# Attention on one core: score products on two half arrays in pairs of heads, and the value products of a group in two bursts

## The chip, the cores and the metric

The kernel is one program on one core of a Trainium2 chip. The metric is the device time of one execution in microseconds (us), the median of several runs. A core has TensorE (matrix products into PSUM), VectorE (DVE), ScalarE (ACT), GpSimd (POOL) and SyncE (SP, which only issues transfers here). They run side by side and meet at semaphores.

## What is computed

Sixteen sequences of 512 tokens with 128 features pass through six residual layers: a small per-channel MLP, attention, the MLP again, routed experts, a gated scan, and the experts again. The change is in the attention layer (and in two details of how the MLP before it stores the keys). Cut to what matters, that layer is:

```python
q = (x @ Wq).reshape(B, S, 16, 8)      # 16 heads of 8 dimensions
k = (x @ Wk).reshape(B, S, 4, 8)       # 4 key heads, each shared by 4 query heads
v = (x @ Wv).reshape(B, S, 4, 8)
q, k = rope(q), rope(k)
att = softmax(causal(q @ k.T * 8 ** -0.5))
x = x + (att @ v) @ Wo
```

## The kernel before, in words

**Parts.** The MLP layer in front splits each fp32 q and k value into three bf16 parts (high, middle, low) and stores them in DRAM (`q_parts`, `k_parts`). A product of q and k is then the sum over all nine pairs of parts: `KQ` = 72 rows of contraction for a head of 8 dimensions. SP loads q three times below itself (line 770) and a copy of k whose rows pair with it (line 772).

**Steps.** `attention` runs over 16 sequences n and, in each, 4 groups g of 4 heads that share a key head. One (n, g) is a step of the loop `step`; there are 64. Every queue is written out by hand and is in order; what an engine has to wait for is a semaphore before the instruction. In a step TensorE works for three groups at once:

- **scores** (`scores`, lines 813 and 815) of the group three steps ahead. For each chunk c of 128 queries and each head: the product q·k over the (c+1)·128 keys that the chunk may see, then a product identity × mask that adds -1e38 to the part above the diagonal. These come in six tiles (`S_TILES`), over two PSUM tiles `at_s_ps` of two banks each. DVE reduces each tile to the negative row maximum (`maxima`, line 1024); tile k waits until tile k-2 is reduced.
- **less_max** (line 825), the group of this step: ten tiles (`X_TILES`) of k·q with keys on the partitions, 512 columns each, with two rows more in the contraction that subtract the maximum (74 rows). They alternate over two banks `at_x_ps`; ACT writes exp of a tile to `at_p` (line 936), and tile i waits until ACT has read tile i-2. POOL sets the entries above the diagonal to zero, every two tiles (line 991).
- **weigh** (line 840), the group one step back: values × probabilities, fp32, with 32 columns of the array for each of the four heads, 32 matrix instructions in one burst. It waits for POOL's last masking of that group.
- **max_rows** (line 848) transposes the maxima of the group two steps ahead; ACT copies, POOL splits them into two bf16 parts, and SP stores and loads them as the two extra rows (lines 777 and 779).
- one of `turn_output`, `turn_normal`, `project` (lines 279, 861, 868) for the output of two groups, over one bank `at_misc_ps`, whose reader is ACT or DVE. It has to be read before `max_rows` may write there again.

The places in the row of ten tiles are numbers: `S_BEFORE` says before which tile each score tile stands, `WEIGH_AT` = 2, `ROWS_AT` = 3, `MISC_AT` = 7 say behind which tile the other pieces stand. ACT and POOL have the same numbers in their loops.

## Time and profile before

| what | value |
|---|---|
| median of 3 runs | 1807.9 us (1804.65 to 1808.93) |
| the profiled execution | 1808.5 us, of which the span of the trace is 1806.8 us |
| mean granted TensorE clock | 0.923 |
| attention, in the trace | about 226 to 860 us |
| its steady part, 300 to 800 us | PE busy 483.3, DVE 357.7, ACT 322.8, POOL 199.1 us; clock 1.00 |

Times in rows are microseconds from the start of the span. PE rows are matrix products, PEld rows are loads of the stationary operand. A product's duration in the trace holds its way through the array as well, so that consecutive products overlap in the rows: what a product costs is the distance from its start to the start of the next one.

### The profile page before, as it was taken

The page shows a single profiled execution, that of the slowest core. Times are in us where ns is not written, and L with a number is a line of the kernel's source. Part 1 is how long each engine was busy: PE and PEld are TensorE (multiplying, and loading weights), DVE is VectorE, ACT ScalarE, POOL GpSimd, SP SyncE. Part 2 cuts the span into 40 slices and gives each one's busy share as a digit, 9 for nine tenths or more (in the row PEclk, how much of TensorE's full clock was granted, in tenths as well). Part 3 has the DMA queues.
Part 4 walks back from the last instruction along what each step waited for, and adds up shares of the span by engine and source line. Part 5 has one row for each costly group of instructions (what it writes and reads, how often), then busy time and mean ns, then how long its engine had stood idle before and what let it go on. Part 6 is the DMA issues. An engine that isn't in the chain of part 4 may idle for free. (4 is left out here: it accounts for less than half of the span.)

```text
span 1806.8 us, 38981 instructions
## 1 busy us (share of the span) xinstructions
PE 1556.2 (86%) x11698; PEld 1092.2 (60%) x11698; DVE 1269.5 (70%) x3160; ACT 1156.7 (64%) x2439; POOL 771.7 (43%) x1202
## 2 busy tenths in 40 slices
PE   3999589999999999997799269999977834999998
PEld 1445245555555555553355159999964524999997
DVE  3787367777777777772786657787768766777776
ACT  3788316666666666665587347877847623788775
POOL 2587614334333444333343456655302203665540
PEclk9999759999999999998899579999989856999999
DMA  5022331111111111100011311111001100111110
GB/s 140 23 70 62 92 75 41 39 43 42 43 43 43 43 42 40 38 19 2 12 36 35 105 28 39 39 32 29 21 1 32 40 24 21 51 49 46 46 44 23
DMA packets 72828, 76.49 MB, mean 42 GB/s; under 512 B 13040, under 2 KB 61488, under 8 KB 72752
## 3 DMA queue, kind: packets, MB, share of 16 engines
q1 hardware_dynamic: 64560, 58.77, 11.2%
q0 software_dynamic: 8192, 16.79, 3.5%
q8 instruction: 37, 0.61, 0.1%
q14 instruction: 39, 0.32, 0.1%
HBM read 51.40 MB, written 24.12 MB: 42 GB/s over the span
## 5 line engine op out<-in xcount | busy, mean ns | idle before, releaser
L1024 DVE TENSOR_REDUCE at_negmax<-at_s_ps 128x2 f32<-128x1024 f32 (+3 forms) x384 | 393.2, 1045 | 170.3 <-PE at_s_ps L815 167.4
L936 ACT ACTIVATE at_p<-at_x_ps 128x512 f32<-128x512 f32 x640 | 353.5, 591 | 158.0 <-PE at_x_ps L825 151.2
L991 POOL TENSOR_SCALAR_AFFINE_SELECT at_p<-at_p 128x256 f32<-128x256 f32 (+1 forms) x448 | 190.8, 438 | 347.5 <-ACT at_p L936 347.5
L1248 POOL DMA_INDIRECT e_x_in<-xn,e_row_c x256 | 259.6, 1014 | 146.0 <-issue 85.0
L813 PE MATMUL at_s_ps<-at_kr,at_qr 72*128 72x512 bf16 (+3 forms) x1024 | 252.9, 312 | 23.2 <-DMA at_kr<-k_parts 20.7
L825 PE MATMUL at_x_ps<-at_qr,at_kr 74*128 74x512 bf16 (+3 forms) x1024 | 235.7, 305 | 22.6 <-ACT at_p L936 12.9
L1369 DVE TENSOR_TENSOR e_hid_lo<-e_hid,e_hid_hi 128x512 fp32r<-128x512 f32 x256 | 177.4, 694 | 83.2 <-ACT e_hid_hi L1333 74.5
L815 PE MATMUL at_s_ps<-maskb,identb 128*128 128x128 bf16 x1024 | 202.1, 225 | 0.0
L1332 ACT ACTIVATE e_hid<-e_h_ps 128x512 f32<-128x512 f32 x256 | 154.7, 604 | 42.1 <-PE e_h_ps L1274 37.4
L840 PE MATMUL at_o_ps<-at_p,at_va 128*32 128x512 f32 (+3 forms) x2048 | 155.5, 445 | 1.6 <-POOL at_p L991 1.6
L1274 PE MATMUL e_h_ps<-e_x_hi,w_hi 128*128 128x256 f32 x512 | 156.6, 306 | 0.0
L1333 ACT ACTIVATE e_hid_hi<-e_h_ps 128x512 fp32r<-128x512 f32 x256 | 155.3, 607 | 0.0
L825 PEld LDWEIGHTS at_x_ps<-at_qr,at_kr 74*128 74x128 bf16 x1024 | 84.6, 98 | 114.7 <-ACT at_p L936 84.2
L813 PEld LDWEIGHTS at_s_ps<-at_kr,at_qr 72*128 72x128 bf16 x1024 | 102.8, 100 | 83.8 <-issue 20.9
L1274 PE MATMUL e_h_ps<-e_x_hi,w_lo 128*128 128x256 f32 x512 | 145.9, 285 | 0.0
L1274 PE MATMUL e_h_ps<-e_x_lo,w_hi 128*128 128x256 f32 x512 | 145.5, 284 | 0.0
L1284 PE MATMUL e_yt_ps<-e_hid_hi,w_lo 128*128 128x256 f32 x512 | 144.3, 282 | 0.0
L1284 PE MATMUL e_yt_ps<-e_hid_hi,w_hi 128*128 128x256 f32 x512 | 144.1, 282 | 0.0
L1284 PE MATMUL e_yt_ps<-e_hid_lo,w_hi 128*128 128x256 f32 x512 | 144.0, 281 | 0.0
L1325 ACT ACTIVATE e_x_hi<-e_t_ps 128x256 fp32r<-128x256 f32 x128 | 49.5, 386 | 135.2 <-PE e_t_ps L1263 124.3
L840 PEld LDWEIGHTS at_o_ps<-at_p,at_va 128*32 128x32 f32 x2048 | 60.8, 111 | 96.2 <-issue 83.1
L1302 PE MATMUL e_acc_ps<-e_hot,e_y_hi 128*128 128x512 f32 x256 | 111.7, 436 | 3.0 <-DVE e_hot L1388 3.0
(196 smaller groups left out, 3495.6 us busy)
## 6 DMA issues: line engine op xcount, KB each, us to landing
at_qr<-q_parts SPq DMA_DIRECT2D x192, 96.0 KB
k_parts<-m_kparts SPq DMA_DIRECT2D x48, 96.0 KB, 1.8
at_kr<-k_parts SPq DMA_DIRECT2D x64, 72.0 KB
xres<-in_x_dram SPq DMA_DIRECT2D x8, 512.0 KB, 7.6
xn<-m_n_xhat SPq DMA_DIRECT2D x16, 256.0 KB
e_x_in<-xn,e_row_c POOLq DMA_INDIRECT x256
xn<-sc_n_xhat SPq DMA_DIRECT2D x16, 256.0 KB
out_dram<-xres SPq DMA_DIRECT2D x16, 256.0 KB
```

Of the source, the lines that this page charges most:

```text
L813: pe.matmul(s_ps[k % 2][:, at:at + w], qr[u][0:KQ, q0:q0 + P], kr[u][0:KQ, g * T:g * T + w], start=True, stop=False)
L815: mm = pe.matmul(s_ps[k % 2][:, at + w - P:at + w], h["identb"][:], h["maskb"][:], start=False, stop=True)
L825: mm = pe.matmul(x_ps[i % 2][:, at:at + T - c * P], kr[u][0:KM, g * T + c * P:g * T + (c + 1) * P], qr[u][0:KM, q0 + c * P:q0 + T], start= ...
L840: mm = pe.matmul(o_ps[32 * j:32 * j + 32, c * P:T], va[u][:, c, g, :], p_sb[g % 2][:, i, at:at + T - c * P], start=(c == 0 and g % 2 == 0) ...
L936: a.activation(p_sb[g % 2][:, i, :], x_ps[i % 2][:], ACT.Exp, scale=SCALE).then_inc(x_read, 1)
L991: sel = gp.affine_select(out=part, in_=part, compare_op=ALU.is_ge, fill=0.0, base=0, pattern=[[0, n] for n in part.shape[1:-1]] + [[1, P]] ...
L1024: v.tensor_reduce(negmax[u][:, h0:h0 + len(heads), c], s_ps[k % 2][:, 0:len(heads) * pitch].rearrange("p (j w) -> p j w", w=pitch)[:, :, 0:w],
L1248: nc.gpsimd.indirect_dma_start(out=x_in[k][u][:], out_offset=None, in_=xn_dram, in_offset=bass.IndirectOffsetOnAxis(ap=row_c[k][:, u:u + 1 ...
L1274: mm = pe.matmul(h_ps[half][:, f, :], w1[:, k, at:at + P], x[k % 2][:], start=(j == 0), stop=(j == len(pairs) - 1))
L1284: mm = pe.matmul(yt_ps[:], w2[:, k, f * D:(f + 1) * D], x[k % 2][:, f, :], start=(f == 0 and j == 0), stop=(f == FC - 1 and j == len(pairs ...
L1333: a.activation(hid_hi[k % 2][:, half * HC:(half + 1) * HC, :], h_ps[half][:], ACT.Gelu).then_inc(gelu_done, 1)
L1369: v.tensor_tensor(hid_lo[k % 2][:, chunks, :], hid[half][:], whole(hid_hi[k % 2][:, chunks, :]), ALU.subtract).then_inc(hl_done, 1)
```

## The change

**Contraction of 48 rows, twice.** Of the nine pairs of parts it keeps six (high with all three, middle with two, low with one), so `KQ` is 48 and `KM` is 50. q is laid out so that the even heads of a group stand at partitions 0 to 49 and the odd ones at 64 to 113, and k stands in both places. A score product now names 48 rows of one half of the array (`HALF` = 64 rows), and products are issued in pairs, one head on each half, which write to two different banks.

**Masks.** The mask product of 128 rows and 128 columns of a head is replaced by two products of 64 rows and 64 columns (`selb` × `maskb`), issued in turn for the two heads of a pair.

**less_max** takes the half by the parity of the tile: even tiles on rows 0 to 49, odd ones on rows 64 to 113. The last two tiles hold heads (0, 2) and (1, 3) instead of (0, 1) and (2, 3).

**weigh** is split in two bursts of 16 instructions: chunks 0 and 3 (512 and 128 columns) behind tile 1, chunks 1 and 2 (384 and 256 columns) behind tile 4. The wait for POOL's masking stands ahead of the first. Before, all 32 stood behind tile 2.

**Other pieces.** `max_rows` moves from behind tile 3 to behind tile 1, ahead of the first burst; the `misc` piece from behind tile 7 to behind tile 8. ACT copies the output of the value products behind tile 4 instead of tile 2.

**Transfers.** SP issues eight loads for a group instead of four (24, 16 and 8 rows of q and 48 of k for each half), and two loads of the maxima instead of one. The bytes of a group go from 360 to 288 KB. The stored copies of k are three of the high part, two of the middle and one of the low.

```diff
-KQ = PARTS * PARTS * HD
+KEPT = [PARTS - j for j in range(PARTS)]
+KFIRST = [sum(KEPT[:j]) for j in range(PARTS)]
+KQ = sum(KEPT) * HD
 KM = KQ + 2
+HALF = P // 2
...
-for copy in range(PARTS):
-    sp.dma_start(k_dram[i * W + b].rearrange("(j c p) t -> c p j t", c=PARTS, p=KR)[copy],
-                 rot["k"]["parts"][b * KR:(b + 1) * KR]).then_inc(parts_out[W], 16)
+rows = k_dram[i * W + b].rearrange("(x p) t -> p x t", p=KR)
+for j, copies in enumerate(KEPT):
+    part = rot["k"]["parts"][b * KR:(b + 1) * KR, j, :]
+    sp.dma_start(rows[:, KFIRST[j]:KFIRST[j] + copies, :],
+                 part.unsqueeze(1).to_broadcast([KR, copies, T])).then_inc(parts_out[W], 16)
...
-          [[(2, 2 * i, 0), (2, 2 * i + 1, 256)] for i in range(GH // 2)]
+          [[(2, i, 0), (2, i + 2, 256)] for i in range(GH // 2)]
 NX = len(X_TILES)
-S_TILES = [(3, (0, 1), 512), (3, (2, 3), 512), (2, (0, 1), 512), (2, (2, 3), 512), (1, (0, 1, 2, 3), 256), (0, (0, 1, 2, 3), 128)]
+S_TILES = [(3, (0, 1)), (3, (2, 3)), (2, (0, 1)), (2, (2, 3)), (1, (0, 1, 2, 3)), (0, (0, 1, 2, 3))]
 NS = len(S_TILES)
 S_BEFORE = {0: 0, 2: 1, 3: 2, 5: 3, 7: 4, 8: 5}
 NG = NKV // 2
 DEN = 2 * HD
-WEIGH_AT, ROWS_AT, MISC_AT = 2, 3, 7
+WEIGH_AT, MISC_AT = (1, 4), 8
+WEIGH_CHUNKS = ((0, 3), (1, 2))
...
-    q = q_dram[n].rearrange("(r h) t -> r h t", h=NH)
+    q = q_dram[n].rearrange("(r g a s) t -> s g r a t", g=NKV, a=2, s=2)
     k = k_dram[n].rearrange("(r h) t -> r h t", h=NKV)
-    rows = PARTS * HD
-    for j in range(PARTS):
-        sp.dma_start(qr[u][j * rows:(j + 1) * rows, g * GH * T:(g + 1) * GH * T].rearrange("r (h t) -> r h t", h=GH),
-                     q[:, g * GH:(g + 1) * GH, :]).then_inc(qk_in[u][g], 16)
-    sp.dma_start(kr[u][0:KQ, g * T:(g + 1) * T], k[:, g, :]).then_inc(qk_in[u][g], 16)
+    for half in range(2):
+        for j, kept in enumerate(KEPT):
+            at = half * HALF + KFIRST[j] * HD
+            sp.dma_start(qr[u][at:at + kept * HD, g * 2 * T:(g + 1) * 2 * T].rearrange("r (a t) -> r a t", a=2),
+                         q[half, g, 0:kept * HD]).then_inc(qk_in[u][g], 16)
+        sp.dma_start(kr[u][half * HALF:half * HALF + KQ, g * T:(g + 1) * T], k[:, g, :]).then_inc(qk_in[u][g], 16)
 def maxima(n, u, r, g):
     sp.wait_ge(m2_done, n * NKV + g + 1)
     sp.dma_start(m_dram[u].rearrange("a r q -> r a q")[g * GH * C:(g + 1) * GH * C], m_parts[g % 2][:]).then_inc(m_stored, 16)
     sp.wait_ge(m_stored, (n * NKV + g + 1) * 16)
-    sp.dma_start(qr[u][KQ:KM, g * GH * T:(g + 1) * GH * T],
-                 m_dram[u].rearrange("a r q -> a (r q)")[:, g * GH * T:(g + 1) * GH * T]).then_inc(m_in[u][g], 16)
+    for half in range(2):
+        sp.dma_start(qr[u][half * HALF + KQ:half * HALF + KM, g * 2 * T:(g + 1) * 2 * T].rearrange("a (x t) -> a x t", x=2),
+                     m_dram[u].rearrange("a (g x s c) q -> s g a x (c q)", g=NKV, x=2, s=2)[half, g]).then_inc(m_in[u][g], 16)
...
-    c, heads, pitch = S_TILES[k]
+        pe.wait_ge(qk_in[u][g], (r + 1) * 2 * (PARTS + 1) * 16)
+    c, heads = S_TILES[k]
     w = (c + 1) * P
     after(pe, s_read, (n * NKV + g) * NS + k - 1)
-    for x, j in enumerate(heads):
-        q0, at = (g * GH + j) * T + c * P, x * pitch
-        pe.matmul(s_ps[k % 2][:, at:at + w], qr[u][0:KQ, q0:q0 + P], kr[u][0:KQ, g * T:g * T + w],
-                  start=True, stop=False)
-        mm = pe.matmul(s_ps[k % 2][:, at + w - P:at + w], h["identb"][:], h["maskb"][:], start=False, stop=True)
+    for a in range(len(heads) // 2):
+        pair = []
+        for half in (first, 1 - first):
+            rows = slice(half * HALF, half * HALF + KQ)
+            q0 = (g * 2 + (heads[0] + 2 * a) // 2) * T + c * P
+            pair.append((slice(half * HALF, (half + 1) * HALF), half * T + a * w))
+            pe.matmul(s_ps[k % 2][:, half * T + a * w:half * T + (a + 1) * w], qr[u][rows, q0:q0 + P],
+                      kr[u][rows, g * T:g * T + w], start=True, stop=False)
+        for x in range(2):
+            for rows, at in pair:
+                at += w - P + x * HALF
+                mm = pe.matmul(s_ps[k % 2][:, at:at + HALF], h["selb"][rows, x * P:(x + 1) * P],
+                               h["maskb"][rows, x * HALF:(x + 1) * HALF], start=False, stop=x == 1)
     mm.then_inc(s_full, 1)
 def less_max(n, u, r, g, i):
     if i == 0:
-        pe.wait_ge(m_in[u][g], r * 16 + 16)
+        pe.wait_ge(m_in[u][g], (r + 1) * 2 * 16)
     after(pe, x_read, (n * NKV + g) * NX + i - 1)
+    rows = slice(i % 2 * HALF, i % 2 * HALF + KM)
     for c, j, at in X_TILES[i]:
-        q0 = (g * GH + j) * T
-        mm = pe.matmul(x_ps[i % 2][:, at:at + T - c * P], kr[u][0:KM, g * T + c * P:g * T + (c + 1) * P],
-                       qr[u][0:KM, q0 + c * P:q0 + T], start=True, stop=True)
+        q0 = (g * 2 + j // 2) * T
+        mm = pe.matmul(x_ps[i % 2][:, at:at + T - c * P], kr[u][rows, g * T + c * P:g * T + (c + 1) * P],
+                       qr[u][rows, q0 + c * P:q0 + T], start=True, stop=True)
     mm.then_inc(x_full, 1)
-def weigh(n, u, g):
-    if g == 0:
-        pe.wait_ge(va_done, n + 1)
-    if g % 2 == 0:
-        after(pe, o_copied, n * NG + g // 2)
-    pe.wait_ge(p_masked, (n * NKV + g) * 5 + 5)
-    order = sorted((c, j, i, at) for i in range(NX) for c, j, at in X_TILES[i])
+def weigh(n, u, g, part):
+    if part == 0:
+        if g == 0:
+            pe.wait_ge(va_done, n + 1)
+        if g % 2 == 0:
+            after(pe, o_copied, n * NG + g // 2)
+        pe.wait_ge(p_masked, (n * NKV + g) * 5 + 5)
+    order = sorted((c, j, i, at) for i in range(NX) for c, j, at in X_TILES[i] if c in WEIGH_CHUNKS[part])
     for c, j, i, at in order:
         mm = pe.matmul(o_ps[32 * j:32 * j + 32, c * P:T], va[u][:, c, g, :], p_sb[g % 2][:, i, at:at + T - c * P],
-                       start=(c == 0 and g % 2 == 0), stop=(c == 3 and g % 2 == 1))
-    mm.then_inc(pv_done, 1)
+                       start=(c == 0 and g % 2 == 0), stop=(c == WEIGH_CHUNKS[1][1] and g % 2 == 1))
+    if part == 1:
+        mm.then_inc(pv_done, 1)
...
-if i == WEIGH_AT and g:
-    weigh(n, u, g - 1)
-elif i == WEIGH_AT and not is_first(n):
-    weigh(n - 1, 1 - u, NKV - 1)
-if i == ROWS_AT and ahead_rows is not None:
+if i == WEIGH_AT[0] and ahead_rows is not None:
     max_rows(*ahead_rows, use(n, g, True))
+if i in WEIGH_AT and g:
+    weigh(n, u, g - 1, WEIGH_AT.index(i))
+elif i in WEIGH_AT and not is_first(n):
+    weigh(n - 1, 1 - u, NKV - 1, WEIGH_AT.index(i))
...
-if i == WEIGH_AT and g == 0 and not is_first(n):
+if i == WEIGH_AT[0] and ahead_rows is not None:
+    copy_rows(ahead_rows[0], ahead_rows[3], use(n, g, True))
+if i == WEIGH_AT[1] and g == 0 and not is_first(n):
     copy_output(n - 1, 1)
-elif i == WEIGH_AT and g == 2:
+elif i == WEIGH_AT[1] and g == 2:
     copy_output(n, 0)
-if i == ROWS_AT + 1 and ahead_rows is not None:
-    copy_rows(ahead_rows[0], ahead_rows[3], use(n, g, True))
...
+scored = s_ps[k % 2][:].rearrange("p (s x) -> p s x", s=2)[:, :, 0:len(heads) // 2 * w]
+if len(heads) == 2:
+    out = negmax[u][:, h0:h0 + 2, c]
+else:
+    scored = scored.rearrange("p s (a w) -> p a s w", w=w)
+    out = negmax[u][:, h0:h0 + GH, c].rearrange("p (a s) -> p a s", s=2)
+v.tensor_reduce(out, scored, AX.X, ALU.max, negate=True).then_inc(s_read, 1)
...
+row, last = at % HALF, at % HALF == HALF - 1
+later = np.where(row[:, None] < np.arange(HALF)[None, :], f32(MASKED), f32(0))
+w["mask"] = np.concatenate([later, np.where(last[:, None], f32(MASKED), later)], 1)
+same = (row[:, None] == np.arange(HALF)[None, :]).astype(f32)
+none = np.zeros((P, HALF), f32)
+w["self"] = np.concatenate([same, none, np.where(last[:, None], f32(1), none), np.where(last[:, None], f32(0), same)], 1)
```

TensorE's queue, behind the first exp tiles of a step (rows ISA and REGISTER_ALU are waits). Before: the third tile (L825), the burst of value products (L840), the next score tile.

```order
L825 MATMUL at_x_ps<-at_qr,at_kr 128x512
L837 ISA
L840 MATMUL at_o_ps<-at_p,at_va 32x512 x4
L840 MATMUL at_o_ps<-at_p,at_va 32x384 x4
L840 MATMUL at_o_ps<-at_p,at_va 32x256 x4
L840 MATMUL at_o_ps<-at_p,at_va 32x128 x4
L286 REGISTER_ALU
L813 MATMUL at_s_ps<-at_kr,at_qr 128x384
```

Now: the first two tiles (L843), the transposed maxima (L868), half of the value products (L859), a score tile as one pair of products (L826) with its four mask products (L831).

```order
L843 MATMUL at_x_ps<-at_qr,at_kr 128x512 x2
L289 ISA
L868 MATMUL at_misc_ps<-pack,at_negmax 16x128
L856 ISA
L859 MATMUL at_o_ps<-at_p,at_va 32x512 x4
L859 MATMUL at_o_ps<-at_p,at_va 32x128 x4
L826 MATMUL at_s_ps<-at_kr,at_qr 128x512 x2
L831 MATMUL at_s_ps<-maskb,selb 128x64 x4
L289 REGISTER_ALU
L843 MATMUL at_x_ps<-at_qr,at_kr 128x512
```

The burst moved ahead by one tile and one score tile, is half as long, and has the transposed maxima in front of it.

TensorE's queue, end of a step. Before: tile 7 (L825), a `misc` piece (L279), and the first head of the last score tile, which three more such pairs of L813 and L815 and tiles 8 and 9 follow.

```order
L825 MATMUL at_x_ps<-at_qr,at_kr 128x384
L825 MATMUL at_x_ps<-at_qr,at_kr 128x128
L853 ISA
L279 MATMUL at_misc_ps<-pack,at_o_t 128x128 x4
L286 REGISTER_ALU
L813 MATMUL at_s_ps<-at_kr,at_qr 128x128
L815 MATMUL at_s_ps<-maskb,identb 128x128
```

Now: the second pair of heads of the last score tile, tile 8, the `misc` piece, tile 9.

```order
L826 MATMUL at_s_ps<-at_kr,at_qr 128x128 x2
L831 MATMUL at_s_ps<-maskb,selb 128x64 x4
L289 REGISTER_ALU
L843 MATMUL at_x_ps<-at_qr,at_kr 128x256 x2
L873 ISA
L282 MATMUL at_misc_ps<-pack,at_o_t 128x128 x4
L289 REGISTER_ALU
L843 MATMUL at_x_ps<-at_qr,at_kr 128x256 x2
```

Eight products of 128 columns became four of 128 columns and eight of 64, and the `misc` piece now stands between the last two exp tiles.

## Rows read from the trace of the kernel before

**Rows 1.** The page: busy time, and granted clock in 40 slices.

```profile
PE 1556.2 (86%) x11698; PEld 1092.2 (60%) x11698; DVE 1269.5 (70%) x3160; ACT 1156.7 (64%) x2439; POOL 771.7 (43%) x1202
...
PEclk9999759999999999998899579999989856999999
```

**Rows 2.** Stretches: length, busy PE, PEld, DVE, ACT, POOL (instructions), clock, DMA share, GB/s.

```profile
300.00:800.00 500.00, 483.34 (x4648) 277.37 (x4646) 357.69 (x420) 322.79 (x638) 199.14 (x515) 1.00 0.14 41
```

**Rows 3.** Waits from 305 to 705 us: in total, times, longest.

```profile
ACT at_p L936 <- PE at_x_ps L825: 101.9, 147, 2.5
PEld at_x_ps L825 <- ACT at_p L936: 56.1, 167, 0.9
```

**Rows 4.** Timeline of PE, one step of 405 to 414 us: start, length, line.

```profile
405.26 0.38 PE L813 MATMUL at_s_ps<-at_kr,at_qr 72*128 72x512 bf16 x1
405.48 0.22 PE L815 MATMUL at_s_ps<-maskb,identb 128*128 128x128 bf16 x1
...
407.16 0.38 PE L825 MATMUL at_x_ps<-at_qr,at_kr 74*128 74x512 bf16 x1
407.47 2.36 PE L840 MATMUL at_o_ps<-at_p,at_va 128*32 128x512 f32 x32
409.77 0.34 PE L813 MATMUL at_s_ps<-at_kr,at_qr 72*128 72x384 bf16 x1
...
412.91 0.60 PE L279 MATMUL at_misc_ps<-pack,at_o_t 128*128 128x128 f32 x4
413.35 0.22 PE L813 MATMUL at_s_ps<-at_kr,at_qr 72*128 72x128 bf16 x1
413.41 0.22 PE L815 MATMUL at_s_ps<-maskb,identb 128*128 128x128 bf16 x1
```

**Rows 5.** The same view: `project`, and the burst four steps later.

```profile
431.39 1.11 PE L868 MATMUL at_misc_ps<-pack,at_o_nt 128*128 128x128 f32 x8
...
444.45 2.36 PE L840 MATMUL at_o_ps<-at_p,at_va 128*32 128x512 f32 x32
```

**Rows 6.** The same view in the scan layer: products on 64 rows and 64 columns.

```profile
1358.76 0.59 PE L1456 MATMUL sc_y_ps<-sc_ts,bmat 64*64 64x512 f32 x1
1359.28 1.09 PE L279 MATMUL sc_xt_ps<-pack,sc_n_xhat 128*128 128x128 f32 x8
...
1389.50 0.59 PE L1455 MATMUL sc_tf_ps<-sc_fg,wlam 64*64 64x512 f32 x1
1389.50 0.59 PE L1456 MATMUL sc_y_ps<-sc_ts,bmat 64*64 64x512 f32 x1
1389.92 0.59 PE L1455 MATMUL sc_tf_ps<-sc_fg,wlam 64*64 64x512 f32 x1
```

**Rows 7.** Timelines of ACT and POOL, start of the same step as Rows 4.

```profile
405.24 2.17 ACT L936 ACTIVATE at_p<-at_x_ps 128x512 f32<-128x512 f32 x4 [0.53 <-PE at_x_ps L825]
...
406.49 0.64 POOL L991 TENSOR_SCALAR_AFFINE_SELECT at_p<-at_p 128x512 f32<-128x512 f32 x1 [0.67 <-ACT at_p L936]
```

**Rows 8.** Timeline, scan layer: eleven products of 8 columns, each with a load.

```profile
1384.48 1.29 PE L249 MATMUL sc_gate_ps<-pack,sc_xhat_t 128*128 128x8 f32 x11
```

**Rows 9.** Stretches, columns as in Rows 2: start of attention, and steps without scores.

```profile
256.00:268.00 12.00, 12.00 (x56) 6.93 (x55) 7.51 (x7) 6.66 (x13) 3.64 (x9) 0.50 0.08 25
268.00:272.00 4.00, 4.00 (x32) 1.17 (x33) 1.23 (x1) 0.81 (x2) 0.41 (x1) 0.62 0.08 27
...
826.80:830.20 3.40, 2.61 (x15) 1.14 (x15) 0.00 (x0) 3.33 (x8) 2.38 (x7) 1.00 0.00 0
830.20:833.60 3.40, 2.91 (x14) 0.80 (x18) 0.00 (x0) 2.08 (x4) 1.20 (x3) 0.59 0.02 5
```

**Rows 10.** Timeline of PE in those steps: two bursts of value products, with idle between.

```profile
823.46 2.36 PE L840 MATMUL at_o_ps<-at_p,at_va 128*32 128x512 f32 x32
...
828.60 0.80 PE L825 MATMUL at_x_ps<-at_qr,at_kr 74*128 74x256 bf16 x4
...
830.65 1.10 PE L825 MATMUL at_x_ps<-at_qr,at_kr 74*128 74x512 bf16 x2 [0.51 <-ACT at_p L936]
831.68 1.94 PE L840 MATMUL at_o_ps<-at_p,at_va 128*32 128x512 f32 x8
```

**Rows 11.** Timelines at the start of attention: SP's first and last loads, the maxima; PE.

```profile
228.14 1.16 SPq L770 DMA_DIRECT2D at_qr<-q_parts  x3
...
241.88 0.36 SPq L772 DMA_DIRECT2D at_kr<-k_parts  x1
248.53 0.33 SPq L777 DMA_DIRECT2D row_max<-at_m_parts  x1
251.03 0.23 SPq L779 DMA_DIRECT2D at_qr<-row_max  x1
...
256.01 1.06 PE L825 MATMUL at_x_ps<-at_qr,at_kr 74*128 74x512 bf16 x2
```

More of the change, by code:

```diff
@@ L707, in attention @@
         s = lambda n: sem(f"at_{n}")
-        qr = [t(f"qr{u}", [P, NH * T], BF16) for u in range(2)]
+        qr = [t(f"qr{u}", [P, NH // 2 * T], BF16) for u in range(2)]
         kr = [t(f"kr{u}", [P, NKV * T], BF16) for u in range(2)]
@@ L875, in step @@
                             if ahead is not None and i in S_BEFORE:
-                                scores(*ahead, S_BEFORE[i])
+                                scores(*ahead, S_BEFORE[i], i % 2)
                             less_max(n, u, r, g, i)
-                            if i == WEIGH_AT and g:
-                                weigh(n, u, g - 1)
-                            elif i == WEIGH_AT and not is_first(n):
-                                weigh(n - 1, 1 - u, NKV - 1)
-                            if i == ROWS_AT and ahead_rows is not None:
+                            if i == WEIGH_AT[0] and ahead_rows is not None:
                                 max_rows(*ahead_rows, use(n, g, True))
+                            if i in WEIGH_AT and g:
+                                weigh(n, u, g - 1, WEIGH_AT.index(i))
+                            elif i in WEIGH_AT and not is_first(n):
+                                weigh(n - 1, 1 - u, NKV - 1, WEIGH_AT.index(i))
                             if i == MISC_AT and g == 3:
@@ L896, in first @@
                         for k in range(NS):
-                            scores(*FIRST, g, k)
+                            scores(*FIRST, g, k, 0)
                         if g:
@@ L903, in flush @@
                     done = use(n, NKV - 1, False) + 1
-                    weigh(n, u, NKV - 1)
+                    for part in range(2):
+                        weigh(n, u, NKV - 1, part)
                     turn_output(n, 1, done)
@@ L1564, in program @@
         q_dram = dram("q_parts", [NB, PARTS * P, T], BF16)
-        k_dram = dram("k_parts", [NB, PARTS * 96, T], BF16)
+        k_dram = dram("k_parts", [NB, KQ * NKV, T], BF16)
         xn_dram = dram("xn", [NB * T, D], F32)
@@ L1633, in layouts @@
     w["pairsum"] = np.tile(np.eye(M, dtype=f32), (2, 2))
-    w["mask"] = np.where(at[None, :] > at[:, None], f32(MASKED), f32(0))
+    row, last = at % HALF, at % HALF == HALF - 1
[4 more added lines that the diff above has]
+    w["self"] = np.concatenate([same, none, np.where(last[:, None], f32(1), none), np.where(last[:, None], f32(0), same)], 1)
     w["iota"] = np.broadcast_to(np.arange(T, dtype=f32), (P, T))
```

14 lines of the change are left out of this document (5 added, 9 removed).

## Prediction, written before the changed kernel had run

> **What bounds it now.** I read the page first: TensorE (PE) has the largest busy share, and its clock is at full speed through the attention layer [rows 1]. In the steady part of that layer PE is busy 483 of 500 us, DVE 358, ACT 323 [rows 2], so PE's queue sets the pace. From one burst of value products to the same burst a sequence later it is 444.45 - 407.47 = 36.98 us, 9.25 us for each of four steps [rows 4, 5]. The table of waits says that it is not PE alone: PE waited for ACT to read a tile (56 us in 400), and ACT for PE (102 us) [rows 3]. They have two banks between them; while PE runs a burst of 2.30 us (407.47 to 409.77, [rows 4]), ACT has two tiles to read, 1.1 us.
>
> **PE's work in a step before.** Distances between starts [rows 4]: a score product costs 0.22 us for 512 columns (405.26 to 405.48) and 0.06 for 128 (413.35 to 413.41), and in proportion between. Four heads of 512, 384, 256 and 128 columns: 4 × 0.56 = 2.2. Sixteen masks of 128 columns: 0.93. Exp tiles, 5120 columns: 2.2. The burst: 2.30. The misc piece is 0.44 (412.91 to 413.35), in one of four steps eight products of 0.11 [rows 5], 0.55 on average; max_rows another 0.11. Sum 8.3, so 0.95 of 9.25 us is waiting.
>
> **What the pairs take away.** Two products on two halves cost as much as one if they run at once. The trace has this in the scan layer: products on the two row halves start in the same hundredth of a microsecond, and the next pair 0.43 us later, the time of one such product alone [rows 6]. They also used different columns; pairs that share all 128 columns are in no row. I take them as parallel: 2.2 becomes 1.1. Exp tiles keep their 2.2, since one tile has one half; about 0.1 of it lies beside products of the other half.
>
> **The masks.** Sixteen products of 128 columns become 32 of 64, in 16 rounds of two. Half of 0.058 is 0.027 a round if columns alone decide; 0.058 if a round cannot be shorter than today's 128-column product; at worst 0.11, the distance at which products of 8 columns follow each other when each has a fp32 load of 128 columns [rows 8]. The masks' bf16 loads kept up with 0.058 before, so the last is far. I take 0.04: 0.64 us a step (0.43 to 0.93; 1.8 at the far end).
>
> The Trainium skill (TensorEngine Tiling (Array Packing), Instruction Overhead) warns against this edit: a product has about 60 cycles of overhead, and a factor should not be taken from a dimension that is already small. By it 64 columns cost what one column does, 32 products one behind the other about 0.8 us, and in rounds of two 0.4; the sum would be 1778 or 1772 by the one or the other. No row here has a 64-column product.
>
> **Changes of mode.** Going from one division of the array to another costs a gap. From the last exp tile (407.16, 0.22 of columns) to the burst (407.47) there are 0.09 us [rows 4], and from 64-row products (1358.76, 0.43 of columns) to a full one (1359.28) also 0.09 [rows 6]. Before, a step had two (into and out of the burst). Now it has seven: halves to full for max_rows, full to burst, burst to halves, halves to burst, burst to halves, halves to full for misc, and back. 7 × 0.095 = 0.67 us against 0.19.
>
> PE's work after: 1.1 + 0.64 + 2.1 + 2.11 (the burst without its gaps) + 0.55 + 0.11 = 6.6, with the gaps 7.3 us.
>
> **What waits remain.** I laid the new order beside the durations, from the first score tile of a step. (a) Tile 1 waits until ACT has read tile 9 of the step before: ACT needs 0.54 us a tile (2.17 for four, [rows 7]) and PE now arrives 0.3 us sooner: 0.34. (b) max_rows stood three tiles in, now one; the bank's last reader (DVE's normalise behind the last reduction, or ACT's copy) and the reduction are only just done: 0.28. (c) The first burst waits for POOL's mask of tiles 8 and 9: POOL started about 0.15 us after ACT's second tile ended and took 0.64 [rows 7]. Before, that was over at 407.13, 0.3 us ahead of the burst. One tile and one score tile earlier it comes last, about 1.4 us into the step: 0.23. (d) Tile 4 waits for ACT, which got tiles 2 and 3 together behind the burst: 0.39. (e) Tile 7 and the last tiles: 0.1 to 0.3. Sum 1.37. The step is 7.3 + 1.37 = 8.65 us. The same walk for the queue before gives 9.17 where the trace has 9.25, so I use the difference, 0.52 us a step, 2.1 a sequence.
>
> Of what the halving frees (1.1 + 0.3 on the masks), 0.5 goes to gaps and 0.4 to waits that move to POOL, DVE and ACT.
>
> **The sum.** The steady part has 15 sequences (280 to 820 us): -31 us. The last three steps have no scores and take 8.2 us from burst to burst (823.46 to 831.68, [rows 10]); with two short bursts ACT idles less: -2. Start: 32 loads took 13.7 us to issue (228.14 to 241.88), 64 take 27 and end near 255.5; the store and load of the first maxima behind them take 2.5 us plus landing [rows 11], so the first exp tile comes near 259 instead of 256.0: +3. The following steps run at half clock, where PE's halved products save about as much: -3. SP in the steady part has 11 issues of about 0.4 us in 8.7: hidden; the maxima have a whole step of slack, and bytes fall. DVE reduces the same elements. Sum -33 us: 1808.5 - 33 = 1775, and the median stands 0.6 us beside the profiled execution, so 1775 for both.
>
> **Rivals.**
>
> *The clock falls (slower).* The clock was at 1.2 GHz from the start of attention while PE was busy without a break with 72- and 74-row products, and rose only with the first burst of fp32 value products on 128 rows [rows 9]; in a step without scores it fell again [rows 9], where PE had idle gaps of 0.5 us and its columns were busy 60% of the step (4.9 of 8.2 us, [rows 10]). So being busy was not enough to raise it, and a looser step lost it. After the change PE's columns are busy 6.6 of 8.65 us, 76%, mostly on 48 or 50 rows: between the 60% that lost the clock and today's 88%. A step at half clock would take about 13.5 us, 4.8 more; one in each sequence costs 15 × 4.8 = 72 us and the time is 1848. It decides from one such step in 2.3 sequences on, where it eats the gain. The short bursts, two in a step, speak against it. The Trainium skill (TensorE: Matmul & The Clock Gate, HAM oscillation) names long idle gaps between bursts as the cause; by that rule the clock stays up and the time is 1775, but the fall in rows 9 had no gap over 0.6 us before it, so I keep this case.
>
> *The halves do not run together*, because they share columns: the products keep 2.2, the masks take 32 × 0.04 = 1.3, and the gaps stay: the walk gives 9.55 us a step against 9.17, 60 × 0.38 = 23 us: 1831.
>
> *Loads bound the masks* at 0.11 a round: 1.76 us a step instead of 0.64. Some of it falls into the waits; the walk then gives 9.08 a step against 9.17, 15 × 4 × 0.09 = 5 us: 1803, no change.
>
> *More than that*: gaps lie inside waits, masks cost 0.03, and (b) and (c) are half as long. Then a step is 8.2 us against 9.17 and the time 1748. DVE (358/500 of 9.25 = 6.6 us) and ACT (6.0) allow it.
>
> **Numbers.** Forecast 1775, with 1756 to 1795 its own range: 0.55. More: 0.13. Load-bound masks or other losses that end within 0.3% (about what a measurement of this kernel can tell from no change, 5.4 us): 0.10. Serial halves: 0.08. Clock: 0.14. Range 1742 to 1820: it takes in the fast rival and the cheap end of the clock's. Faster 0.68, same 0.11, slower 0.21.
>
> **What would show it.** Two L826 products in the same hundredth of a microsecond, the next pair 0.22 behind: pairs are right; at twice that they are serial. Mask rounds 0.03 to 0.06 apart. Gaps of 0.09 at seven places. A sequence of 34.9 us instead of 37.0. The first burst released by POOL L991 or its mask, max_rows by DVE. A clock of 1.00 from 280 to 820; anything less there and the forecast fails on the clock. It also fails if the waits grow where I have 1.37.

## The result, and the profile after

The changed kernel took 1812.1 us (median of 20 runs, 1808.1 to 1816.5), the one before 1808.1 beside it (20 runs, 1803.2 to 1811.7). The ratio is 1.0025, with a 95% interval of 1.0017 to 1.0034: nothing gained, where 33 us were forecast. The profiled execution took 1812.2 us (span 1810.5; before 1808.5 and 1806.8).

The page of the changed kernel: busy time, clock in 40 slices, and the queue q8, which moves code (experiments 1 to 4 show that it is PE's):

```profile
PE 1465.9 (81%) x12722; PEld 1011.2 (56%) x12722; DVE 1261.6 (70%) x3160; ACT 1159.9 (64%) x2439; POOL 767.4 (42%) x1202
...
PEclk9999758999999999997899579999988856999999
...
q8 instruction: 85, 1.39, 0.3%
```

PE is busy 90 us less than in [rows 1], and the end has not moved. Queue q8 carried 85 packets of 16 KB; before it was 37 (0.61 MB). That queue was on the page of the kernel before as well, and no step of the prediction had read it.

Stretches of the changed kernel (columns as in [rows 2]):

```profile
300.00:364.00 64.00, 53.60 (x757) 28.43 (x753) 46.70 (x55) 43.68 (x86) 25.96 (x68) 1.00 0.15 37
364.00:373.50 9.50, 6.15 (x48) 2.29 (x45) 3.74 (x7) 2.85 (x7) 2.91 (x8) 0.64 0.12 32
373.50:440.00 66.50, 55.67 (x777) 29.24 (x774) 48.69 (x57) 45.67 (x90) 27.02 (x71) 1.00 0.14 35
```

Most of the time the clock is 1.00 as forecast, and PE is filled less than before. In between lies a stretch of 9.5 us in which the clock is lower and all engines do little. Timeline of PE there:

```profile
363.87 0.39 PE L843 MATMUL at_x_ps<-at_qr,at_kr 50*128 50x256 bf16 x2
364.19 0.66 PE L282 MATMUL at_misc_ps<-pack,at_o_t 128*128 128x128 f32 x4
364.78 0.39 PE L843 MATMUL at_x_ps<-at_qr,at_kr 50*128 50x256 bf16 x2
368.51 0.61 PE L826 MATMUL at_s_ps<-at_kr,at_qr 48*128 48x512 bf16 x2 [3.35 <-issue]
```

PE stands still for 3.35 us and its releaser is "issue": it waited for nothing that the profile shows. The place is the end of the body of PE's loop over two images (the trace has a compare-and-branch at 364.5, then at 440.1, 515.3, 590.6, 665.4 and 740.7; behind the first five PE idles 3.0 to 3.4 us, behind the last, which leaves the loop, it does not). The same in the table of waits from 305 to 705 us (in total, times, longest), against [rows 3]:

```profile
ACT at_p L957 <- PE at_x_ps L843: 130.7, 112, 3.9
...
PEld at_x_ps L843 <- ACT at_p L957: 64.4, 123, 0.6
...
PEld at_s_ps L826 <- issue: 28.2, 51, 3.7
...
PE at_s_ps L826 <- issue: 16.1, 5, 3.4
```

Sixteen microseconds in five waits of PE; before, no such wait was there. From within or just behind each of the five the granted clock was half for 3.4 or 6.8 us (366.5 to 373.3, 441.5 to 448.4, 516.6 to 523.5, 595.1 to 598.6, 666.8 to 673.7).

What the two together cost is in the distances between the first bursts of successive steps. Timeline of PE, two first bursts, four steps (a sequence) apart:

```profile
388.96 1.28 PE L859 MATMUL at_o_ps<-at_p,at_va 128*32 128x512 f32 x16 [0.18 <-POOL at_p L1012]
...
424.34 0.64 PE L859 MATMUL at_o_ps<-at_p,at_va 128*32 128x512 f32 x4 [0.18 <-POOL at_p L1012]
```

An undisturbed sequence is 424.34 - 388.96 = 35.38 us, 1.6 less than the 36.98 of [rows 4, 5]: without the stalls the 58 steps from the third on that still have scores would have been 22.9 us shorter than before. Around the first stall the two distances are 357.97 to 369.90 and 369.90 to 380.13, 11.93 + 10.23 us, where the steps without a stall take 8.68 + 8.68: 4.8 us more. At the other four it is 4.4, 4.6, 4.0 and 4.5, in all 22.4. Nearly the whole gain went there.

At the end, the last three steps (without scores) took 30.3 us from burst to burst, 25.4 before, at a mean clock of 0.74 against 0.91. At the start the first burst came 3.4 us earlier (265.53), but the clock fell again from 274.3 to 284.5 and took 3.1 us back.

### The profile page after: what moved, and what is told of

Its sections match the earlier page's. It is cut to its first block and busy times, and to the rows that moved or that the text cites. A ratio compares the mean times of both kernels' runs of the same rounds, so it can differ in the third digit from the quotient of the medians.

```text
span 1810.5 us, 41589 instructions
## 1 busy us (share of the span) xinstructions
PE 1465.9 (81%) x12722; PEld 1011.2 (56%) x12722; DVE 1261.6 (70%) x3160; ACT 1159.9 (64%) x2439; POOL 767.4 (42%) x1202
## 5 line engine op out<-in xcount | busy, mean ns | idle before, releaser
L1051 DVE TENSOR_REDUCE at_negmax<-at_s_ps 128x2 f32<-128x1024 f32 (+3 forms) x384 | 383.9, 1042 | 174.6 <-PE at_s_ps L831 174.2
L843 PE MATMUL at_x_ps<-at_qr,at_kr 50*128 50x512 bf16 (+3 forms) x1024 | 209.6, 308 | 81.4 <-ACT at_p L957 75.4
L826 PE MATMUL at_s_ps<-at_kr,at_qr 48*128 48x512 bf16 (+3 forms) x1024 | 174.7, 316 | 43.6 <-DMA at_kr<-k_parts 20.9
L859 PE MATMUL at_o_ps<-at_p,at_va 128*32 128x512 f32 (+3 forms) x2048 | 178.0, 469 | 14.1 <-POOL at_p L1012 13.9
L831 PE MATMUL at_s_ps<-maskb,selb 64*128 64x64 bf16 x2048 | 138.3, 194 | 0.0
L831 PEld LDWEIGHTS at_s_ps<-maskb,selb 64*128 64x128 bf16 x2048 | 111.2, 99 | 34.0 <-issue 7.5
L843 PEld LDWEIGHTS at_x_ps<-at_qr,at_kr 50*128 50x128 bf16 x1024 | 60.3, 95 | 121.1 <-ACT at_p L957 103.3
L859 PEld LDWEIGHTS at_o_ps<-at_p,at_va 128*32 128x32 f32 x2048 | 56.6, 114 | 111.7 <-issue 89.5
```

Of the source, the lines that this page charges most:

```text
L826: pe.matmul(s_ps[k % 2][:, half * T + a * w:half * T + (a + 1) * w], qr[u][rows, q0:q0 + P], kr[u][rows, g * T:g * T + w], start=True, sto ...
L831: mm = pe.matmul(s_ps[k % 2][:, at:at + HALF], h["selb"][rows, x * P:(x + 1) * P], h["maskb"][rows, x * HALF:(x + 1) * HALF], start=False, ...
L843: mm = pe.matmul(x_ps[i % 2][:, at:at + T - c * P], kr[u][rows, g * T + c * P:g * T + (c + 1) * P], qr[u][rows, q0 + c * P:q0 + T], start= ...
L859: mm = pe.matmul(o_ps[32 * j:32 * j + 32, c * P:T], va[u][:, c, g, :], p_sb[g % 2][:, i, at:at + T - c * P], start=(c == 0 and g % 2 == 0) ...
L1051: v.tensor_reduce(out, scored, AX.X, ALU.max, negate=True).then_inc(s_read, 1)
```

## The experiments

Three theories stood at first. **A**: the body of PE's loop has outgrown what PE keeps of its code, so each jump back waits for code. **B**: the clock falls because the new products give the array less to do, and the place is chance. **C**: the stall waits for a load of data. All kernels compute the reference but the fourth, which leaves out part of its masks. Times are medians; ratios are to the kernel before on the same chip, with 95% intervals. The kernel before took 1807.0 us beside experiments 1 to 4, 1808.1 beside 5 to 8 and 1806.9 beside 9 to 12, which puts about 1 us between times of different groups.

**1. PE's loop written out** (the other engines keep theirs).

```diff
-            with eng.Fori(0, NB // 2 - 2) as i:
-                step(i * 2 + 1, 1, i)
-                step(i * 2 + 2, 0, i + 1)
-            for n in range(NB - 3, NB):
-                step(n, n % 2, n // 2)
+            if eng is unrolled:                 # PE alone
+                for n in range(1, NB):
+                    step(n, n % 2, n // 2)
+            else:
...
```

> The changed kernel, computing the same, with one edit: TensorE's queue alone has the fourteen middle images of the attention layer written out in place of its loop of two images; the other engines keep theirs. In the changed kernel's trace TensorE stood idle for 3.0 to 3.4 us behind the branch at the end of each of the first five turns of its loop (at 365.2, 440.7, 515.9, 591.2 and 666.0 us), its clock fell within the next microseconds, and the two burst distances around each stall were 21.3 to 22.2 us together instead of 17.4. Theory A (the body of the loop has outgrown what TensorE keeps of its code: the instruction queue q8 moved 48 more packets than before, and each jump back must wait for code): no branch, no stall, no fall of the clock between 290 and 820 us; q8 still carries the code, hidden. Five times 4.8 us come back: 1812 - 24 = 1788 us (1784 to 1792), faster than before by 1.1%. Rival B (the clock falls by the shorter products themselves, and the loop's end only marks the time): the falls stay somewhere in each 75 us, the stall alone goes, five times 3.2 less what the half clock adds to nothing: 1800 or more. Rival C (the stall waits for a load, not for code): it stays where it was, before the first score product of the same image: 1812.

1796.6 us, ratio 0.9936 (0.9922 to 0.9949): between A's 1784 to 1792 and B's 1800. The stalls are gone, with the 22.4 us around them, and since the loads are as they were, C falls. Between 290 and 800 us one fall of the clock is left, at 455.2. So the stall hung on the jump, and most of the falls in the middle came with it. What kept the time from A's 1788 is the end. Stretch of the last three steps, in the kernel before and here:

```profile
823.40:848.90 25.50, 19.65 (x163) 8.09 (x165) 1.54 (x4) 16.65 (x32) 9.57 (x23) 0.91 0.01 2
```

```profile
803.70:840.40 36.70, 29.22 (x159) 9.39 (x160) 1.54 (x4) 16.74 (x32) 9.56 (x23) 0.50 0.01 2
```

They take 36.7 us at half clock instead of 25.5 (30.3 in the changed kernel). No jump is near, which is what B says; experiment 5 tests it. A sequence is also 0.19 us longer than in the loop (35.56 us), as it is in the changed kernel's own last images behind its loop; why, the runs don't say (the kernel before, written out, keeps its 36.98).

**2. The kernel before, written out** the same way.

> The kernel before with the same edit: TensorE's queue written out for the middle images, the other engines unchanged. Its loop showed no stall at its end, and q8 carried no packet between 372.7 and 756.7 us. Theory A: nothing to win, within 0.3% of before (1803 to 1813), and q8 now shows packets all through the layer with no idle time of TensorE beside them. Rivals B and C say the same of this kernel. If it is slower, streaming of code has a price of its own, which would also stand in the first experiment; if it is faster by more than 0.3%, the loop cost something that the trace of before did not show.

1807.7 us, 1.0005 (0.9993 to 1.0017). Code that streams in costs nothing (28 packets of q8 between 373 and 757 us, no idle time of PE with them), and its loop cost nothing either. Two images have 1408 PE entries in this trace, so in those 384 us PE ran some 7300, about 260 for each packet of 16 KB.

**3. The kernel before with a longer body.**

```diff
-                        mm = pe.matmul(s_ps[...][:, at + w - P:at + w], h["identb"][:], h["maskb"][:], ...)
+                        for x in range(2):
+                            mm = pe.matmul(s_ps[...][:, at + w - P + x * 64:at + w - P + (x + 1) * 64],
+                                           h["identb"][:], h["maskb"][:, x * 64:(x + 1) * 64], ...)
```

> The kernel before, computing the same, with each mask product of 128 columns split into two of 64 columns on the whole array: 32 products a step instead of 16, so that the loop body of TensorE gets 256 entries longer (a product and its weight load each), from about 1540 that the trace shows to about 1795, near the 1827 of the changed kernel. Nothing runs on halves. Theory A: stalls of 3.0 to 3.4 us at each of five jumps back, q8 with about nine packets in each turn, and falls of the clock if the stall is what brings them. Masks themselves cost between nothing (two of 0.027 for one of 0.057) and 16 x 0.03 = 0.5 us a step, 30 us. So 1808 + 24 = 1832 with the falls, 1824 without, plus up to 30. Rival B: the clock stays at 1.00, since the rows are as before, and no stall: 1808 to 1838 by the masks alone. Rival C: no stall.

1837.2 us, 1.0177 (1.0161 to 1.0192). Without one product on a half array, the same stalls are there, 3.3 to 3.7 us behind the same five jumps, and the clock falls at each. Two masks of 64 columns cost what one of 128 did (undisturbed sequence 37.07 us). Timeline of PE at the first jump, after its branch at 365.6:

```profile
369.51 0.39 PE L813 MATMUL at_s_ps<-at_kr,at_qr 72*128 72x512 bf16 x1 [3.38 <-issue]
```

Counted exactly between two branches, a turn has 1526 PE entries in the trace before, 1782 in the changed kernel and here (the texts on record, which counted from a window, have all of these 13 to 45 higher).

**4. The changed kernel with a shorter body**, half of its mask products left out.

```diff
-                        for x in range(2):
+                        for x in (1,):
                             for rows, at in pair:
```

> The changed kernel with its loop kept and half of the mask products left out (the ones for the first 64 of the 128 columns of each diagonal block), so that the maxima of those rows are taken over scores that should be hidden: part of the computation is missing and the output is not the reference's. The body gets 256 entries shorter, from about 1827 to about 1571. Theory A: no stall at the jumps, q8 silent between 373 and 757 us, clock 1.00 there; 24 us from the stalls and up to 60 x 8 x 0.03 = 14 us from the rounds left out (less where DVE and ACT set the pace): 1774 to 1788. Rival B: the clock still falls in each turn, now with even fewer products: 1798 or more. Rival C: stalls stay: 1798 to 1812.

1810.7 us, 1.0019 (1.0008 to 1.0030): nothing gained, though the turn has 1526 entries again and no stall (q8 silent from 373 to 735 us, as in the kernel before). The clock was half in 16 stretches of mostly 3.4 us between 290 and 830 us, and a step that met one took some 1.5 us more (10.2 to 10.7 instead of 8.6 to 9.1). So the forecast of A alone (1774 to 1788) failed, and B's price (1798 or more) was met: with still less for the array to do, the clock falls with no stall near. The two mechanisms are separate. Experiment 3 had the stalls with nothing on halves, this one the falls with no stall.

**5. Written out, with the halves filled up.** The idea (D, in the text on record) is that rows count for the array's work as well as columns. The added rows hold zeros in the queries and ones in the keys.

```diff
-KM = KQ + 2
+KP = HALF - 2                                # 62; rows KQ..KP of the queries stay zero
+KM = HALF
...
-                        sp.dma_start(qr[u][half * HALF + KQ:half * HALF + KM, ...
+                        sp.dma_start(qr[u][half * HALF + KP:half * HALF + KM, ...
...
-                            rows = slice(half * HALF, half * HALF + KQ)     # scores
+                            rows = slice(half * HALF, half * HALF + KP)
...
+                    for u in range(2):                                       # POOL, first()
+                        gp.memset(qr[u][:].bitcast(F32), 0.0).then_inc(qr_set, 1)
```

> The first experiment's kernel with the halves filled up, computing the same: the two rows of the maxima stand at rows 62 and 63 of each half, and the rows between hold zero in the queries, so that score products use 62 rows and exp products 64 instead of 48 and 50. No product has more columns and none is added, so no work of TensorE gets longer at a given clock. In the first experiment's trace the stalls were gone, yet the clock was half at 274.3 to 284.5, 455.2 to 458.6, 803.4 to 844.4 us, and the last three steps took 11.87, 12.92 and 11.86 us against 8.22, 9.69 and 7.49 of the kernel before. Theory D (the clock falls where TensorE's array does too little for too long, and rows that multiply zeros count as work done): the falls inside 290 to 840 us go, the steps of the end take 8 to 9 us: -11 for the end, -3 for the start, -1.4 for the one at 455: 1781 us (1778 to 1786). Rival E (only busy time counts, rows don't): the same falls, 1797. Rival F (the falls follow where the array switches between halves and whole): the same falls, 1797.

1782.7 us, 0.9865 (0.9848 to 0.9883), 14 us less than experiment 1. The clock is 1.00 from 270 to 805 us, and the last three steps take 27.8 us, not 36.7:

```profile
270.00:805.00 535.00, 444.37 (x6086) 232.39 (x6084) 385.25 (x461) 362.97 (x711) 221.46 (x577) 1.00 0.13 34
```

```profile
797.10:824.90 27.80, 19.83 (x162) 7.12 (x162) 1.54 (x4) 16.68 (x32) 9.53 (x23) 0.88 0.01 2
```

The products and their columns are the same, only on 62 and 64 rows instead of 48 and 50, and PE's busy time from 300 to 700 us is the same 333.4 us. E (rows don't count) and F (the changes of mode bring the falls) fall. It is not one trace's luck: the mean granted clock of every run is 0.923 to 0.928 here and 0.913 to 0.917 in experiment 1. The same holds for the changed kernel (0.910 to 0.915 in 20 runs) against experiment 6 (0.917 to 0.925 in 10), and for experiment 10 against 7. But filling does not hold the clock everywhere: it fell from 805.6 to 812.4 us here, and in experiment 7 the last three steps ran at 0.61.

**6. Filled, loop kept.**

> The changed kernel, loop kept, with the same filling of the halves as in the run before. The body stays as long as in the changed kernel (about 1827 entries in the trace). Theory A with D: the five stalls of 3.0 to 3.4 us stay, since code is what they wait for, and the clock falls after them or not by what the filled rows give back: with falls 1812 less the start's 3, less 4 for the end: 1805; without falls at the stalls also 5 x 1.6 = 8 us less: 1797. Rival E: 1812.

1802.7 us, 0.9971 (0.9958 to 0.9985). All five stalls stay, 3.1 to 3.5 us, and the clock fell at each: the filled rows don't carry it over 3 us of standing still. Against experiment 5 the loop costs 20 us.

**7. The pairs alone**, filled and written out: value products in one burst behind the third tile again, max_rows and the misc piece where they were before.

```diff
-WEIGH_AT, MISC_AT = (1, 4), 8
-WEIGH_CHUNKS = ((0, 3), (1, 2))
+WEIGH_AT, ROWS_AT, MISC_AT = (2, None), 3, 7
+WEIGH_CHUNKS = ((0, 1, 2, 3), ())
```

> The filled and written-out kernel of the first of these runs with the value products back in one burst behind the third exp tile, max_rows behind the fourth and the misc piece behind the eighth, as in the kernel before: the pairs alone, computing the same. Four changes of mode a step fewer would be two fewer (0.19 us), and the waits for POOL's mask and at max_rows (0.23 and 0.28 in the forecast) go; ACT stands idle through a burst of 2.1 us instead, with two tiles to read, 1.1 us. If the split of the burst is what lets the pairs' time be used, a step is 0.3 to 0.5 us longer than the 8.89 us of the first experiment (15 sequences of four: +18 to +30, 1799 to 1811). If the two split bursts only cost gaps and waits, this is faster: 8.6 us a step, 1764. I expect the first.

1767.4 us, 0.9768 (0.9746 to 0.9790). I had expected the other way. Timeline of PE, bursts four steps apart:

```profile
408.97 0.64 PE L867 MATMUL at_o_ps<-at_p,at_va 128*32 128x512 f32 x4
...
443.53 0.64 PE L867 MATMUL at_o_ps<-at_p,at_va 128*32 128x512 f32 x4
```

34.56 us a sequence, against 35.54 in experiment 5: the two bursts, with what moved beside them, cost 0.24 us a step.

**8. The bursts alone**, in the kernel before.

> The kernel before with the other part of the change alone: the value products in two bursts behind exp tiles 2 and 5, max_rows behind tile 2, the misc piece behind tile 9; score products whole. PE's work grows by two changes of mode, 0.19 us a step, and its waits can shrink by no more than the 0.95 us that they are. In the forecast's steps the waits (a) 0.34, (c) 0.23 and (d) 0.39 follow from PE coming too early; with the long score products it comes later. Between -0.4 and +0.2 us a step: 1784 to 1820; I take the middle, 1802.

1806.3 us, 0.9994 (0.9984 to 1.0005). The sequence is 37.31 us instead of 36.98, so two bursts cost 0.08 us a step there (why three times as much with the pairs, no run says), and the steps without scores take 24.6 us instead of 25.4. The half of the change that was to give the pairs' time an outlet was no gain with them or without.

**9. Work for the array in the last three steps.**

```diff
+                def fill(n, u, g, i):         # where there are no scores
...
+                    rows = slice((1 - i % 2) * HALF, (2 - i % 2) * HALF)
+                    pe.matmul(s_ps[i % 2][:, 0:T], kr[u][rows, 0:P], qr[u][rows, 0:T], start=True, stop=True)
...
                             less_max(n, u, r, g, i)
+                            if ahead is None:
+                                fill(n, u, g, i)
```

> The kernel of the pairs alone (one burst, TensorE's queue written out, halves filled), with work for the array in the last three steps, which have no scores: beside each of their exp tiles one product of 64 rows and 512 columns on the other half, into a score bank that nobody reads any more. It computes the same. In the run without it the clock was half at 788.5 to 795.3, 798.7 to 819.2 and 822.6 to 836.3 us and the last three steps took 10.26, 11.77 and 11.17 us, where the kernel before had 8.22, 9.69 and 7.49. Theory D (the clock falls where the array does too little): the falls from 788 on go, the three steps take 8.3 to 9, so 8 us less: 1759 (1756 to 1763). The products on the other half run beside the exp tiles and cost nothing by themselves. Rival E (what matters is busy time or the waits alone): the falls stay, 1767; and if the extra products don't run beside, 30 x 0.22 = 6.6 us more, 1774.

1764.9 us, 0.9768 (0.9752 to 0.9784). The profiled executions of experiment 7 and of this one, the last three steps:

```profile
781.10:814.40 33.30, 26.86 (x163) 9.38 (x166) 1.54 (x4) 16.60 (x32) 9.53 (x23) 0.61 0.01 2
```

```profile
782.70:807.50 24.80, 18.76 (x191) 7.87 (x193) 1.54 (x4) 16.56 (x32) 9.53 (x23) 1.00 0.01 2
```

And PE's timeline in the second (L860 is the filler, L851 the exp tile on the other half):

```profile
793.35 0.39 PE L851 MATMUL at_x_ps<-at_qr,at_kr 64*128 64x512 bf16 x1
793.35 0.60 PE L860 MATMUL at_s_ps<-at_qr,at_kr 64*128 64x512 bf16 x2
```

More products, and the stretch is 8.5 us shorter, at a clock of 1.00. The fillers start with the exp tiles and run beside them. Yet the ratio is that of experiment 7, not the 8 us less that were expected: the four runs of experiment 7 spread from 1762.2 to 1772.3, and the profiled one was the slowest, with a mean granted clock of 0.921, where the other three had 0.925, 0.925 and 0.928. With fillers it was 0.926 to 0.929 in all five runs. That fillers help in the mean is not shown; that they hold the clock in the traced execution is.

**10. The pairs alone, not filled.**

> The pairs alone, one burst, TensorE's queue written out, but the halves not filled: score products on 48 rows and exp products on 50. Against the filled one (1767.4) this prices the filling where PE's columns are busy for more of each step. Theory D: more falls than the five of the filled one, above all at the start (268 to 290) and from 780 us on: 5 to 15 us more, 1772 to 1782. Rival E: the same falls, 1767.

1782.1 us, 0.9865 (0.9847 to 0.9882): 15 us more than filled, with falls at 273.7, 311.3, 417.1, 557.0 and 697.0 and four around the end, and a mean clock of 0.914 to 0.917 in its four runs. About the price between experiments 1 and 5 (14 us).

**11. The pairs alone, filled, loop kept.**

> The pairs alone with filled halves, but with TensorE's loop of two images kept; the body is again about 1810 entries in the trace. Theory A: five stalls of 3.0 to 3.5 us at the jumps back, with a fall of the clock behind each as in the filled kernel with two bursts (11.9 + 10.2 us there instead of 17.4): 5 x 4.8 = 24 us more than written out: 1791. If the denser step holds the clock through a stall: 5 x 3.2 = 16, 1783. That the stall belongs to the two bursts: 1767.

1796.8 us, 0.9947 (0.9926 to 0.9968), 6 more than expected. The five stalls are 3.7 to 4.2 us here and the two distances around one take 12.3 to 12.8 and 8.9 to 10.5 us, without one 8.4 and 8.4: in all 29 us more than written out. So the jumps alone take almost three quarters of what the pairs, filled and written out, are worth (41 us).

**12. The kernel before, body in between** (masks split where score products have 384 or 512 columns).

> The kernel before, computing the same, with the mask products split in two only where the score products have 512 or 384 columns: 8 more products a step, so 128 entries more in the body, about 1667, between the 1571 that showed no stall and the 1795 that did. It bounds the length from which a jump back costs. If the limit lies below 1667: five stalls of 3 to 3.6 us, q8 with eight or nine packets a turn, some 1828 us. If above: none, q8 silent between 373 and 757 us, 1808 to 1812. I lean to the second, since TensorE keeps whole blocks of 16 KB and seven of those are 1792 entries.

1849.8 us (one run), the worst of all, and I had leaned to no stall, on the ground that seven blocks of 16 KB would hold the body; that ground was wrong. The turn has 1654 entries, and its trace accounts for the time: 41 us more than before in the 58 steps with scores from the third on, some 8 at each jump. PE's timeline behind the jump at 367.6:

```profile
371.30 0.60 PE L813 MATMUL at_s_ps<-at_kr,at_qr 72*128 72x512 bf16 x1 [3.10 <-issue]
...
372.23 0.26 PE L817 MATMUL at_s_ps<-maskb,identb 128*128 128x64 bf16 x1
374.49 0.24 PE L817 MATMUL at_s_ps<-maskb,identb 128*128 128x64 bf16 x1 [2.00 <-issue]
```

It stalls twice, and so at all five jumps: 3.1 to 3.3 us, then, a few products on, 1.9 to 2.5 more. q8's packets come at 368.7 and 371.8. The likely reading is that code comes in packets of 16 KB and this jump lands near the end of one; that reading was not tested. What is shown: 1526 entries a turn jump back free, 1654 do not, and the price does not simply grow with the length (1782 stall once).

## Why the prediction was wrong

It forecast 1775 us; the time was 1812, inside the range (1742 to 1820), but 4 us slower instead of 33 faster. That the range holds it is luck: it reached up to 1820 for a clock that falls by itself, and not for stalls. By its steps:

**The pairs: right.** Pairs of score products start 3 ns apart and share all 128 columns. PE's timeline of the changed kernel, one step:

```profile
405.18 0.22 PE L831 MATMUL at_s_ps<-maskb,selb 64*128 64x64 bf16 x2
405.24 0.38 PE L843 MATMUL at_x_ps<-at_qr,at_kr 50*128 50x512 bf16 x1
...
406.03 0.39 PE L843 MATMUL at_x_ps<-at_qr,at_kr 50*128 50x512 bf16 x1 [0.41 <-ACT at_p L957]
406.35 0.28 PE L868 MATMUL at_misc_ps<-pack,at_negmax 128*16 128x128 f32 x1
406.83 1.28 PE L859 MATMUL at_o_ps<-at_p,at_va 128*32 128x512 f32 x16 [0.20 <-POOL at_p L1012]
408.04 0.39 PE L826 MATMUL at_s_ps<-at_kr,at_qr 48*128 48x512 bf16 x2
408.27 0.22 PE L831 MATMUL at_s_ps<-maskb,selb 64*128 64x64 bf16 x4
408.33 0.38 PE L843 MATMUL at_x_ps<-at_qr,at_kr 50*128 50x512 bf16 x1
...
409.40 0.39 PE L843 MATMUL at_x_ps<-at_qr,at_kr 50*128 50x384 bf16 x2 [0.46 <-ACT at_p L957]
```

Two products of 512 columns in 408.04 to 408.27, four masks in 0.06 us.

**The masks: right in kind, a little dear.** A round took 0.03 us, not 0.04: 0.48 us a step for 0.64.

**The changes of mode: right.** 0.092 to 0.105 us at each, forecast 0.095 (406.03 + 0.21 of columns to 406.35 is one).

**The waits: mis-sized, 2.0 us for 1.37.** In the table of waits from 305 to 705 us PE waits for ACT to read an exp tile far more than before (changed kernel, then the kernel before):

```profile
PE at_x_ps L843 <- ACT at_p L957: 49.6, 123, 0.5
```

```profile
PE at_x_ps L825 <- ACT at_p L936: 6.5, 11, 0.6
```

From the rows of the one step above, less the columns of the product ahead: (a) to 406.03, 0.56 for 0.34; (b) nothing for 0.28; (c) to 406.83, 0.28 for 0.23, by POOL as forecast; (d) to 409.40, 0.63 for 0.39; (e) 0.50 at tile 6 (at 403.55) for 0.1 to 0.3. PE's own work was less than the 7.3 taken (masks, and score pairs that run beside an exp tile of one half), so the step came out at 8.84 us on average for 8.73 (9.25 less the 0.52): 22.9 us for the 31 forecast. Here the walk compared the change only with the kernel before. It never walked the pairs with the old single burst, which took 8.64 us a step in experiment 7.

**The start: right in sum** (the first exp tile came at 257.4, 1.4 us late and not 3; by the first burst 3.4 us were won, and the fall of the clock at 274.3 took 3.1 back). **The end: wrong**, +4.9 us for -2, by the clock. The text took 8.2 us for a step there; the three took 8.2, 9.7 and 7.5 before.

**The failed step: "a clock of 1.00 from 280 to 820".** The text named it as the one on which it fails, and gave the falling clock 0.14. It had two things wrong. The first is a term that was not in the sum: the change adds 16 mask products a step to a loop of eight steps, 256 entries a turn with their loads, and PE waits 3.0 to 3.4 us for code at each jump; stalls and the falls of the clock with them took 22.4 us. The trace before had the sign of it: q8 silent from 373 to 735 us. The Trainium skill (Runtime: NRT & Kernel Launch, Instruction fetch mechanics) says that "Branching breaks sequential prefetch" when the target is not among the two pages held; the traces agree on the stall, but the loop of 1526 entries, six such pages, jumped back free, so PE keeps more than two. The same section of the Trainium skill gives PE room for 2048 instructions; a turn of 1654 was too long here. I weighed neither sentence before. The second is that the rival counted columns and put the danger in every sequence. In the changed kernel the falls came with the stalls, at the start and in the steps without scores; everywhere else in its steady part the clock held. Its price was too high as well: in experiment 4 a step wholly at half clock (273.26 to 285.30) took 12.0 us for 8.6, 3.4 more, where the rival had 4.8. The Trainium skill (TensorE: Matmul & The Clock Gate, HAM oscillation) names long idle gaps as the cause. For the falls at the stalls the traces agree, with 3.0 to 4.2 us of standing still behind the jump in five kernels. For the others they do not: experiments 1 and 5 have the same products and the same steps at full clock, differ in rows, and 14 us lie between them.

The sum as it came out, from first burst to last: start -0.3, steady steps -22.9, stalls and the falls with them +22.4, end +4.9: +4.1 at the last burst, +3.7 between the profiled executions.

## What to carry to other kernels

Count what an edit adds to a hardware loop's body on each engine, not only what it takes from the busy time, and look at the code queue: if it is silent in the loop and the body grows, write the loop out first (it cost nothing in the kernel before, 0.19 us a sequence in the changed one) and measure then. When products are made smaller, the clock becomes a term of the sum; here the unused rows could be filled, with zeros in one operand, at no price in time. And undo the second half of a two-part change by itself: here the pairs alone, written out and filled, gave 1767 us (-2.3%), and the half that was to help them took 15 us.

## What the runs showed of the hardware that I had not expected

- PE's jump back is free at 1526 entries a turn and stalls it for 3.0 to 3.7 us at 1782 (3.7 to 4.2 in experiment 11); at 1654 it stalls for 3.1 to 3.3 and again for 1.9 to 2.5. The 14 images written out came in without a wait.
- In all five kernels with such stalls the clock was half for 3.4 to 10.2 us from within or just behind each of them.
- Going from 48 and 50 rows to 62 and 64, the added ones holding zeros in the queries, took away falls of the clock worth some 14 us in two pairs of kernels, with the same count of products and columns.
- Products of 64 columns on 64 rows follow each other in rounds of two every 0.028 to 0.033 us, with a weight load for each.
